# A Newton iteration carried through y = P² − 3.5P: its linear term moved into a matmul accumulator, half remainders dropped, engine orders rewritten

## The reference, cut to what matters

```python
def iterative_inv(mat, n_iter=6):
    I = jnp.eye(m, dtype=mat.dtype)
    K = mat
    denom = jnp.max(jnp.sum(K, axis=-2), axis=-1)[:, :, None, None]
    V = jnp.swapaxes(K, -1, -2) / denom
    for _ in range(n_iter):
        KV = jnp.matmul(K, V)
        V = jnp.matmul(0.25 * V, 13 * I - jnp.matmul(KV, 15 * I - jnp.matmul(KV, 7 * I - KV)))
    return V
...
kernel1, kernel2, kernel3 = softmax(Q @ K_l'), softmax(Q_l @ K_l'), softmax(Q_l @ K')
SV = jnp.matmul(jnp.matmul(kernel1, iterative_inv(kernel2)), jnp.matmul(kernel3, V))
```

## Time and profile before

| | |
|---|---|
| median of 3 runs | 2021.92 us (2021.71 to 2022.61) |
| profiled execution: span, first to last instruction | 2016.8 us, 5.1 us under the median of the runs |
| busy over the span | TensorE 1789.7 us (89%), VectorE 1700.4 (84%), ScalarE 1081.8 (54%), GpSimd 918.8 (46%) |
| one block of the Nyström phase in its steady state | 27.54 us |
| busy in that block | TensorE 25.48 us, VectorE 24.97, ScalarE 18.22, GpSimd 11.80 |
| granted TensorE clock in that block | 1.00 (2.4 GHz) |

### The profile page before, as it was taken

One profiled execution on the slowest core, in us unless ns is written; L12 is line 12 of the kernel. 1 busy time (PEld: TensorE's weight loads), 2 busy tenths in 40 slices (PEclk: granted clock), 3 DMA queues, 4 the chain that ended last, 5 costly groups with the idle time before them and its releaser, 6 DMA issues.

```text
span 2016.8 us, 66873 instructions
## 1 busy us (share of the span) xinstructions
PE 1789.7 (89%) x27593; PEld 1374.2 (68%) x27593; DVE 1700.4 (84%) x4108; ACT 1081.8 (54%) x2880; POOL 918.8 (46%) x953
## 2 busy tenths in 40 slices
PE   5998999998999688868999999999999999957887
PEld 4887566665888466656777777777777777745666
DVE  5786899998566699957999999999989999867997
ACT  2444333332444466645666666666666666636664
POOL 1000788886000277733444444444444444426886
PEclk9999999999999899978999999999999999988999
DMA  4000000000000000000000000000000000000001
GB/s 120 1 1 1 1 1 2 1 2 1 1 1 1 0 1 1 1 1 3 3 3 3 3 3 4 3 3 3 3 4 3 4 3 3 3 2 1 22 22 43
DMA packets 14606, 14.49 MB, mean 7 GB/s; under 512 B 1440, under 2 KB 12128, under 8 KB 14304
## 3 DMA queue, kind: packets, MB, share of 16 engines
q1 hardware_dynamic: 11104, 8.83, 1.5%
q10 hardware_dynamic: 3200, 1.37, 0.3%
HBM read 6.01 MB, written 4.19 MB: 5 GB/s over the span
## 4 chain that ended last, share of the span: by engine, by line
PE 43%; DVE 40%; issue 8%; ACT 7%; POOL 1%; DMA 1%; DVEq 0%; POOLq 0%; SPq 0%; ACTq 0%
PE acc L515 6%; PE acc L492 6%; DVE arena L620 5%; DVE arena L1290 4%; DVE arena L1282 4%; PE acc L1809 3%; PE acc L1799 3%; DVE arena L615 2%; DVE acc L938 2%; DVE arena L951 2%; PE acc L1821 2%; DVE arena L1321 2%; DVE arena L928 2%; PE acc L801 2%; PE acc L506 2%
## 5 line engine op out<-in xcount | busy, mean ns | idle before, releaser
L1628 POOL TENSOR_TENSOR arena<-arena 128x288 f32<-128x288 f32 (+1 forms) x384 | 269.7, 706 | 461.6 <-ACT arena L1507 380.4
L975 POOL TENSOR_TENSOR arena<-arena 128x960 f32<-128x960 f32 (+2 forms) x74 | 177.6, 2400 | 301.5 <-DVE arena L944 204.8
L1507 ACT ACTIVATE arena<-acc 64x288 f32<-64x288 f32 x384 | 155.3, 405 | 166.6 <-PE acc L1827 86.9
L723 POOL TENSOR_TENSOR arena<-arena,quadcol 128x512 f32<-128x512 f32 x64 | 79.2, 1256 | 240.5 <-DVE arena L590 240.5
L465 ACT ACTIVATE arena<-acc,wib 128x256 f32<-128x256 f32 x256 | 100.3, 474 | 150.9 <-PE acc L506 150.9
L1282 DVE SCALAR_TENSOR_TENSOR arena<-arena,acc 64x256 f32<-64x256 f32 x384 | 161.2, 420 | 14.4 <-PE acc L1827 2.3
L1290 DVE SCALAR_TENSOR_TENSOR arena<-acc,arena 128x288 f32<-128x288 f32 (+1 forms) x384 | 156.3, 407 | 18.1 <-PE acc L1821 10.9
L1821 PEld LDWEIGHTS acc<-arena 64*64 64x64 f32 x3072 | 112.0, 133 | 83.7 <-issue 76.4
L1821 PE MATMUL acc<-arena 64*64 64x72 f32 (+1 forms) x3072 | 136.8, 224 | 35.1 <-DVE arena L1290 29.4
L1799 PE MATMUL acc<-arena 64*64 64x72 f32 x3072 | 138.5, 229 | 16.5 <-DVE arena L1290 11.4
L1061 PE MATMUL acc<-wguT,arena 128*128 128x352 f32 x256 | 106.4, 499 | 48.8 <-DVE arena L928 47.8
(11 more groups left out here) (242 smaller groups left out, 4780.4 us busy)
## 6 DMA issues: line engine op xcount, KB each, us to landing
out_dram<-X SPq DMA_DIRECT2D x3, 1024.0 KB, 5.4
out_dram<-X SPq DMA_DIRECT2D x1, 512.0 KB, 3.2
wi<-in_wiT_dram ACTq DMA_DIRECT2D x1, 256.0 KB, 6.5
wout<-in_woT_dram ACTq DMA_DIRECT2D x1, 256.0 KB, 9.0
out_dram<-X SPq DMA_DIRECT2D x1, 256.0 KB, 2.3
out_dram<-X SPq DMA_DIRECT2D x2, 128.0 KB, 2.5
wqkv<-in_w_qkv_dram ACTq DMA_DIRECT2D x1, 192.0 KB, 9.0
arena<-in_w_down_dram SPq DMA_DIRECT2D x1, 176.0 KB, 4.6
```

What stands on the lines that cost most here:

```text
L975: pool.tensor_tensor(b3(y[k][:, part(u)]), b3(z[k][:, part(u)]), each(small[u % kept][:, 1, blocks(u)]), ALU.mult).then_inc(y_ready, 1)
L1507: act.mul(sq[s][rows, group[1], :], pn[s][other, group[1], 0:MW], 15.0 / (13.0 * size[it]))\
L1628: pool.tensor_tensor(tm[s][:, group[g], cols], pm[s][:, group[g], cols], sq[s][:, group[g], cols], ALU.subtract).then_inc(tm_ready, 1)
```

## The change

The polynomial is rewritten with y = P² − 3.5P, in which P⁴ − 7P³ + 15P² − 13P = y² + 2.75y − 3.375P.

For group 1, `cross` first adds −3.5P in the accumulator by two matmuls with a scaled identity (`eye`) as weights and all 288 columns of a half of the group as moving data; P² is then accumulated on top. ScalarE's two half copies bring y to `sq`, and `cube` becomes `sq` by `sq`. VectorE's two half remainders go.

For group 0, VectorE's `remainder` makes y in one pass of 128x288 from the accumulator and P, GpSimd takes it off a scaled copy of P, which ScalarE now makes from P itself (in SBUF, no longer from the accumulator), and `cross` multiplies y by y. New constants keep the scales, and at the start of the phase GpSimd makes the six scaled identities and a second set of memsets.

The orders of all four engines are rewritten. The core of the diff:

```diff
-            rm = [cut(NP, LM) for _ in R]
+            rm = [cut(NP // 2, MW) for _ in R]
+            eye = cut(NITER, LM)
...
                 def remainder(n, s, it):
-                    iterate(dve, n, it, 0)
-                    dve.wait_ge(sq_ready, turn(n, it, 0))
-                    dve.scalar_tensor_tensor(rm[s][:, group[0], :], pm[s][:, group[0], 0:LM], 7.0 * size[it],
-                                             pn[s][:, group[0], 0:LM], ALU.mult, ALU.subtract).then_inc(rm_ready, 1)
-                def remainder_half(n, s, it, h):
-                    rows, other = halves[h][0], halves[1 - h][0]
...
-                    dve.scalar_tensor_tensor(rm[s][rows, group[1], :], pm[s][rows, group[1], 0:LM], 7.0 * size[it],
-                                             pn[s][other, group[1], 0:LM], ALU.mult, ALU.subtract).then_inc(rm_ready, 1)
+                    dve.wait_ge(sq_done, step(n, it, 0))
+                    dve.scalar_tensor_tensor(rm[s], pn[s][:, group[0], 0:MW], 1.0 / (3.5 * fall[it]),
+                                             pm[s][:, group[0], :], ALU.mult, ALU.subtract).then_inc(rm_ready, 1)
...
                 def square(n, s, it):
-                    act.wait_ge(sq_done, step(n, it, 0))
-                    act.mul(sq[s][:, group[0], :], pn[s][:, group[0], 0:MW], 15.0 / (13.0 * size[it]))\
-                       .then_inc(sq_ready, 1)
+                    cols = slice(LM if it == NITER - 1 else 0, MW)
+                    iterate(act, n, it, 0)
+                    act.mul(sq[s][:, group[0], cols], pm[s][:, group[0], cols], 27.0 / 77.0).then_inc(sq_ready, 1)
...
                 def square_half(n, s, it, h):
                     act.wait_ge(sq_done, step(n, it, 1))
-                    if h == 1:
-                        act.wait_ge(rm_ready, turn(n, it, 1))
...
                 def cross(n, s, it):
-                    pe.wait_ge(sq_ready, turn(n, it, 0))
-                    pe.wait_ge(rm_ready, turn(n, it, 0))
                     iterate(pe, n, it, 1)
+                    for (rows, _), (other, _) in zip(halves, halves[::-1]):
+                        pe.matmul(pn[s][other, group[1], 0:MW], eye[rows, it, :], pm[s][rows, group[1], :], start=True,
+                                  stop=False, skip_group_check=True)
+                    pe.wait_ge(rm_ready, lone(n, it))
                     for p in range(PG):
                         for rows, _ in halves:
-                            mm = pe.matmul(pn[s][rows, p, cols], rm[s][rows, p, :], sq[s][rows, p, cols],
+                            mm = pe.matmul(pn[s][rows, p, cols], rm[s][rows, p, 0:LM], rm[s][rows, p, cols],
                                            start=True, stop=True, skip_group_check=True)
...
-                            mm = pe.matmul(pn[s][other, r, 0:MW], pm[s][rows, r, 0:LM], pm[s][rows, r, :], start=True,
+                            mm = pe.matmul(pn[s][other, r, 0:MW], pm[s][rows, r, 0:LM], pm[s][rows, r, :], start=False,
```

More of the change, by code:

```diff
@@ L1405, in v @@
                     if head:
-                        columns(n + 1, o)
+                        largest(n + 1, o)
+                        spread(n + 1, o)
                     if run:
                         newton(n, s, 3, 0)
[L1409 to L1413, removed]
                     if head:
@@ L1416, in v @@
                     if run:
+                        newton(n, s, 3, 1)
                         remainder(n, s, 4)
[L1418 to L1421, removed]
                         max1(n, s, 0)
-                        remainder_half(n, s, 4, 1)
+                        max1(n, s, 1)
                         newton(n, s, 4, 0)
-                        remainder_half(n, s, 4, 0)
-                        max1(n, s, 1)
+                        lower1(n, s, 0)
                     if fore:
@@ L1504, in square_half @@
                     act.wait_ge(sq_done, step(n, it, 1))
-                    if h == 1:
-                        act.wait_ge(rm_ready, turn(n, it, 1))
-                    act.mul(sq[s][rows, group[1], :], pn[s][other, group[1], 0:MW], 15.0 / (13.0 * size[it]))\
+                    act.mul(sq[s][rows, group[1], :], pn[s][other, group[1], 0:MW], 22.0 / (27.0 * rise[it]))\
                        .then_inc(sq_ready, 1)
@@ L1569, in a @@
                         exp3(n + 1, o, 1)
+                        turned2(n + 1, o)
                     if run:
                         square(n, s, 3)
[L1572 to L1575, removed]
+                        square_half(n, s, 3, 0)
+                        square_half(n, s, 3, 1)
                     if head:
                         turned_kv(n + 1, o)
[L1578 to L1581, removed]
                     if fore:
@@ L1584, in a @@
                     if run:
+                        square(n, s, 4)
                         square_half(n, s, 4, 0)
@@ L1652, in g @@
                     head, fore = 0 <= n + 1 < NB, 0 <= n + 2 < NB
+                    if head:
+                        expand_k(n + 1, o)
                     if run:
@@ L1921, in t @@
                         turned1(n - 1, o, 1)
-                        cube(n - 1, o, 5, 1)
                     if head:
                         scores2(n + 1, o)
+                    if tail:
+                        cube(n - 1, o, 5)
                     if run:
@@ L1928, in t @@
                         back(n - 1, o)
+                    if run:
+                        multiply(n, s, 1, 0)
+                        cube(n, s, 0)
                     if head:
@@ L1931, in t @@
                     if run:
-                        multiply(n, s, 1, 0)
-                        cube(n, s, 0, 1)
+                        cross(n, s, 1)
                     if tail:
                         product(n - 1, o)
-                    if run:
-                        cross(n, s, 1)
-                    if tail:
                         totals(n - 1, o)
```

109 lines of the change are left out of this document (54 added, 55 removed).

## The result

The changed kernel takes 2001.47 us (median of 4 runs, 1999.48 to 2003.96) against 2021.82 for the kernel before: a ratio of 0.9913, 95% interval 0.9889 to 0.9936. It is faster by about 18 us by this ratio (20 by the two medians), where 13 us slower was forecast.

What follows compares the result with a forecast made beforehand. The prediction took PE and VectorE as nearly full, with PE's work deciding after the change: 25.62 + 2.88 − 0.55 = 27.95 us a block against 27.54, +13 us over 32 blocks, 2035 us; range 2018 to 2061.

Steps and rivals of the forecast that it cites:

- the first term of the sum: PE's work per block in the kernel before: 27.54 us less 1.92 of waits, 25.62 us.
- these gaps count as work here: PE's recurring gaps at weight shape changes, 0.15 us each, and slow transpose hand-overs, taken as work.
- The waits of the kernel before: PE's four gaps longer than like ones, put down to VectorE: 1.92 us a block, 61 us in all.
- Half remainders gone, VectorE no longer sets the time: VectorE's busy time falls from 24.97 to about 20.1 us a block; worth at most 1.92 us.
- The pair, 0.48 us each, +2.88: Two identity matmuls added to each `cross` on PE, six times per block, 0.24 to 0.96 us each.
- New order, −0.55: PE's five fewer weight shape changes save 0.75 us a block; one transpose standing alone adds 0.2.
- Waits of the new order near zero: PE's waits for other engines in the rearranged block: 0.0 to 0.1 us, only iteration 2 tight.
- The sum: A block of 27.95 us against 27.54: +0.41, times 32 is +13 us, 2035 us in all.
- the faster one: Pair half hidden, and PE gaps really waits for VectorE: likelier 27.15 us a block, 2009 us; 10%.
- The bank rule: The identity matmuls on PE take turns at one PSUM bank: another 2.88 us a block, about 2127 us; 2%.
- The ScalarE chain: Steps through ScalarE from `turned3` to the third iteration's `cross` decide: block 28.55 us, 2054 us; 21%.

Runs made afterwards that it cites:

- VectorE relieved: Kernel before without its two half remainders per iteration, quartic term of group 1 dropped, order unchanged: block 26.05 us, median 1966.8 us, ratio 0.975.
- the run in the old order: New arithmetic with the step order of the kernel before on all four engines: block 27.75 us, median 2022.3 us, ratio 1.000.
- A second pair: Changed kernel with two more identity-shaped matmuls, weights zero, in each `cross`: block 29.83 us, median 2085.5 us, ratio 1.034.
- the run with columns later: Changed kernel with `newton` and `remainder` ahead of `columns` on VectorE, and its transpose behind the third `cross` on PE: block 26.71 us, median 1990.8 us, ratio 0.987.

## Why the prediction was wrong

**The step that failed is the first term of the sum, PE's own work of 25.62 us, where the runs show 25.0**, and in it the choice to count the slow hand-overs of transposes as work ("these gaps count as work here: they recur without a wait", 0.54 for two transposes). They recurred because a wait for VectorE recurred. PE of the kernel before, at two such places (L1777 and L1737 are transposes, L1799 `multiply`):

```profile
1199.14 0.33 PE L1737 MATMUL acc<-ident,arena 128*128 128x128 f32 x1
1199.51 0.72 PE L1799 MATMUL acc<-arena 64*64 64x72 f32 x16
...
1207.45 0.40 PE L1777 MATMUL acc<-ident,arena 128*128 128x128 f32 x2
1207.95 0.47 PE L1799 MATMUL acc<-arena 64*64 64x72 f32 x8
```

and VectorE's `newton` (L1290) of the same kernel, on which these `multiply` wait:

```profile
1198.99 0.46 DVE L1290 SCALAR_TENSOR_TENSOR arena<-acc,arena 128x288 f32<-128x288 f32 x1
...
1207.44 0.46 DVE L1290 SCALAR_TENSOR_TENSOR arena<-acc,arena 128x288 f32<-128x288 f32 x1 [0.28 <-PE acc L1821]
```

They end at 1199.45 and 1207.90, and `multiply` starts 0.06 and 0.05 later. No idle time is printed on the PE rows, because the modelled end of the last transpose lies only 0.04 and 0.10 before. The rows of the weight loads, which the prediction did not read, do print it:

```profile
1199.51 0.57 PEld L1799 LDWEIGHTS acc<-arena 64*64 64x64 f32 x16 [0.23 <-DVE arena L1290]
...
1207.95 0.57 PEld L1799 LDWEIGHTS acc<-arena 64*64 64x64 f32 x16 [0.34 <-DVE arena L1290]
```

Against the changed kernel's 0.37 for two transposes, and 0.26 for one (measured with VectorE relieved), the hand-overs of `turn_m3`, `turn_w`, `turn_x` and `turn_mx` in the block of the earlier trace rows hid 0.10 + 0.14 + 0.17 + 0.17 = 0.58 us. The waits of the kernel before were 1.92 + 0.58 = 2.50, its own work 25.04; the run in the old order puts it at 24.96. Three of the four shrank when only the arithmetic was new; the one behind `turn_w`, where `newton` still ended 0.05 before, shrank with the new order. The first steps of `cube`, which has one wait fewer now, gave nothing: they follow `multiply` after 0.55 in both.

Point by point:

- *Half remainders gone, VectorE no longer sets the time:* right. VectorE is at 20.5 us, and its relief alone is worth 1.49 us a block in the old order.
- *The pair, 0.48 us each, +2.88:* right for four of the six, 0.47; the first and last cost 0.30 in the old order, so the term is 2.49 there and was put 0.39 too high. (A second pair costs 2.70 in the new order; counted so, the pair takes 0.2 more and the order saves 0.2 more.) Each runs on both its quarters at once. The Trainium skill (TensorEngine Tiling (Array Packing), Restrictions and Gotchas, PSUM pressure) states that different row tiles cannot access the same PSUM bank simultaneously. The trace does not bear it out here: taking turns would have made a pair 0.96, and it is 0.47. The first `cross` has its pair partly beside the `cube` ahead of it, on different quarters; the changed kernel's PE shows the records of both mixed (L1791 `cube`, L1800 the pair):

```profile
1216.26 0.46 PE L1791 MATMUL acc<-arena 64*64 64x8 f32 x10
1216.52 0.46 PE L1800 MATMUL acc<-arena 64*64 64x288 f32 x2
1216.57 0.32 PE L1791 MATMUL acc<-arena 64*64 64x8 f32 x6
```

- *New order, −0.55:* near −0.62, but partly by luck. The 0.62 hold 0.30 of waits that the old order had and 0.42 about `columns` that the new one has; without both, the order is worth 27.45 − 26.71 = 0.74 (27.75 less 0.30, and 27.13 less 0.42), close to the 0.75 that five changes of shape were put at. Which of the moves saved it was not separated.
- *Waits of the new order near zero:* too low. They were 0.42 us a block, about `columns`, as the run with columns later shows.
- *The sum:* 24.96 + 2.49 − 0.74 + 0.42 = 27.13, terms cut from the measured blocks, against 25.62 + 2.88 − 0.55 + 0.0 = 27.95. With the first term alone put right the forecast would have been 27.29, on the right side of 27.54; with the pair alone put right, 27.56.
- *The rivals:* the faster one named this very cause, hand-overs that are waits, at 27.15 us a block, and was given 10%. That it comes within 0.02 of the measured block is luck: its four times 0.2 was 0.58, and other terms made up the rest. What was held against it, that the gap recurs whoever waits, was the error: I had not looked at what VectorE finished just before each of these starts. The bank rule did not hold here. The ScalarE chain was there, at 0.4 us; the gain is what is left beside it.

What was not seen at all is that the pair also fills a wait. The forecast treated PE's work as a plain sum, with a wait in `cross` for the remainder met in time. In the changed kernel that is true only because the pair runs first: with it behind the wait the block is 28.45, without it 26.82. In the sum this cancels, but a reader who asked what the pair costs would have said 2.7 us and been right upward and wrong downward.

## What to carry to other kernels

Before calling a recurring gap an engine's own work, look at what ended on the other engines in the 0.1 us before each of its ends: a wait can hide under the modelled end of a matmul and show no idle time on its row. The row of its weight load can show it. When work moves from a full engine to another nearly full one, the outcome hangs on that second engine's true floor, and an error of 2% in it decides the sign. Work that needs less than its neighbours and can run ahead of a wait costs less than its length while the wait is there (here 0.31 in the new order and 1.71 in the old one, of some 2.5); taking such work away, or putting it behind the wait, shows what it really covered.

## What the runs showed of the hardware

A long matmul pair on two off-diagonal quarters of the array runs beside short ones on the diagonal quarters also across the border of two program steps, as the mixed records at 1216.52 show. A step with 64x64 weights that follows two 128x128 transposes starts 0.37 us after the first of them when nothing makes it wait (1207.68 to 1208.05), and 0.26 after a single one. The weight load of such a step shows the wait where the matmul's own row does not: 0.34 us of idle time ahead of it at 1207.95, where `newton` made it wait, against 0.17 behind two transposes without a wait:

```profile
1206.53 0.19 PEld L1791 LDWEIGHTS acc<-arena 64*64 64x64 f32 x4 [0.17 <-issue]
```
